# Attention scores read from the 32 rows of each head instead of from zero-padded keys of 128 rows

## What is computed

```python
N_HEADS = 16                      # hs = 128 // 16 = 8 features a head
Q, K, V = proj(Wq, bq), proj(Wk, bk), proj(Wv, bv)
Q, K = _apply_rope(Q, cos, sin), _apply_rope(K, cos, sin)
scores = jnp.einsum('bhqd,bhkd->bhqk', Q, K) * (1.0 / jnp.sqrt(hs))
scores = jnp.where(causal, scores, -10000000000.0)
...
```

## Time and profile before

| | |
|---|---|
| time, median of 3 runs | 1768.23 us (1767.26 to 1769.22) |
| time of the profiled execution | 1769.27 us |
| its span, first to last instruction | 1767.2 us |
| PE / DVE / ACT / POOL busy share of the span | 69% / 58% / 36% / 29% |
| mean granted TensorE clock, share of 2.4 GHz | 0.814 |

### The profile page before, as it was taken

How to read it: one execution, slowest core, us unless ns; L and a number is a source line. 1 busy time by engine, 2 the same in 40 slices (tenths; PEclk the granted TensorE clock), 3 DMA queues, 4 the chain that set the end, 5 groups by cost and what they waited for, 6 DMA issues and landing times. The chain is left out here.

```text
span 1767.2 us, 26688 instructions
## 1 busy us (share of the span) xinstructions
PE 1212.8 (69%) x9140; PEld 801.2 (45%) x9214; DVE 1021.9 (58%) x2340; ACT 629.5 (36%) x989; POOL 510.0 (29%) x571
## 2 busy tenths in 40 slices
PE   4625977959635059704888998899889997412991
PEld 2413856839524059702343443344434443311991
DVE  5855555655426136446777776777777770630662
ACT  4632221222111023201265664665566665001330
POOL 2434013040026747712003000300120000374772
PEclk9666988969755579955699998999999998555995
DMA  1439611020120133160000010001000100213325
GB/s 45 155 145 390 266 37 59 0 95 0 36 63 28 53 106 99 52 185 6 7 19 7 10 46 8 7 7 43 8 7 8 31 7 13 62 53 90 98 68 162
DMA packets 109057, 114.06 MB, mean 65 GB/s; under 512 B 8720, under 2 KB 90512, under 8 KB 108048
## 3 DMA queue, kind: packets, MB, share of 16 engines
q1 hardware_dynamic: 96608, 91.98, 16.5%
q0 software_dynamic: 9216, 19.02, 3.2%
q10 hardware_dynamic: 3120, 1.57, 0.3%
HBM read 49.34 MB, written 59.02 MB: 61 GB/s over the span
## 5 line engine op out<-in xcount | busy, mean ns | idle before, releaser
L1829 DVE TENSOR_REDUCE att_mx<-att_ps 128x1 f32<-128x512 f32 (+3 forms) x768 | 405.2, 555 | 146.9 <-PE att_ps L1722 111.3
L1603 ACT ACTIVATE att_prob<-att_ps 128x1024 f32<-128x1024 f32 (+3 forms) x384 | 300.3, 812 | 228.9 <-PE att_ps L1734 176.7
L1719 PE MATMUL att_ps<-att_kT,att_q1T 128*128 128x512 bf16 (+3 forms) x709 | 235.1, 344 | 50.5 <-DVE att_mx L1829 34.2
L1731 PE MATMUL att_ps<-att_q2T,att_kT 128*128 128x512 bf16 (+3 forms) x753 | 201.1, 331 | 3.2 <-ACT att_prob L1603 1.2
L1719 PEld LDWEIGHTS att_ps<-att_kT,att_q1T 128*128 128x128 bf16 x768 | 74.2, 98 | 259.1 <-DVE att_mx L1829 211.7
L978 POOL DMA_INDIRECT sides<-moe_ys,moe_back_i x160 | 153.2, 958 | 87.6 <-issue 47.3
L1745 PE MATMUL att_pso<-att_prob,att_v 128*32 128x512 f32 (+3 forms) x1536 | 163.9, 499 | 1.6
L972 POOL DMA_INDIRECT slots<-moe_rows,moe_place_i x128 | 123.2, 963 | 59.4 <-issue 38.4
L1499 POOL CAST att_qm_rows<-att_nm 128x32 bf16<-128x32 f32 x48 | 15.6, 324 | 395.8 <-DVE att_nm L1838 391.6
L1722 PE MATMUL att_ps<-att_mask,att_identb 128*128 128x128 bf16 x512 | 115.8, 228 | 2.3 <-DVE att_mx L1829 1.5
L1071 PE MATMUL moe_ps_t<-moe_ident,moe_xs 128*128 128x128 f32 x160 | 27.0, 290 | 115.2 <-DMA moe_xs<-slots 115.2
(11 more groups left out here) (283 smaller groups left out, 2439.5 us busy)
## 6 DMA issues: line engine op xcount, KB each, us to landing
slots<-fw_zeros SPq DMA_DIRECT2D x2, 5200.0 KB, 30.1
moe_xs<-slots SPq DMA_DIRECT2D x16, 650.0 KB, 4.9
sides<-fw_zeros SPq DMA_DIRECT2D x2, 4096.0 KB, 35.3
moe_side<-sides SPq DMA_DIRECT2D x16, 512.0 KB, 6.2
tok<-prep_tok SPq DMA_DIRECT2D x4, 1536.0 KB, 5.4
turned<-prep_tT SPq DMA_DIRECT2D x4, 1536.0 KB, 8.7
fw_tok<-tok SPq DMA_DIRECT2D x4, 1536.0 KB, 10.4
fw_Tkv<-turned SPq DMA_DIRECT2D x4, 1024.0 KB, 6.7
```

The lines of the kernel that those rows point to most:

```text
L1603: nc.scalar.activation(prob[(2 * n + pair) % 4][:, :, 0:size], ps2[pair][:, :, 0:size], ACT.Exp, scale=SCORE_SCALE).then_inc(exp_done, 1)
L1719: last = nc.tensor.matmul(out[:, 0:size], q1T[t % 2][:, j * P:(j + 1) * P], kT[t][h][:, 512 * c:512 * c + size], start=True, stop=not diag ...
L1731: last = nc.tensor.matmul(ps2[pair][:, h, 0:size], kT[t][2 * pair + h][:, i * P:(i + 1) * P], q2T[t % 2][:, first:first + size], start=Tru ...
L1829: nc.vector.reduce_max(mx[:, c, j, h:h + 1], ps1[(n * QUAD + h) % 2][:, 0:size], AX.X).then_inc(max_done, 1)
```

## The change

The padded tiles, their zeroing, `kT_all` and the four transfers go. `kT[t]` is one tile of 128 rows that ACT writes directly, and a score matmul names 32 partitions of it and of the queries, so that it is a matmul of 32 rows. In the max pass the heads come in the order 2, 0, 3, 1. In `exp_step` the two score matmuls of a pair come first, then the two masks. The mask matmuls keep their 128 rows.

```diff
-        kT = [[sb(f"kT{s}{h}", [P, SEQ], BF16) for h in range(QUAD)] for s in range(HEADS // QUAD)]
-        kT_all = sb("kT_all", [P, SEQ], BF16)
+        kT = [sb(f"kT{s}", [P, SEQ], BF16) for s in range(HEADS // QUAD)]
...
+        TURNS = (2, 0, 3, 1)
+
+        def head_rows(h):
+            return slice(32 * h, 32 * h + 32)
...
-            def place_keys(count, t):
-
-                wait(sp, misc_free, 1 + count + 1)
-                for h in range(QUAD):
-                    rows = slice(32 * h, 32 * h + 32)
-                    sp.dma_start(kT[t][h][rows, :], kT_all[rows, :]).then_inc(k_placed, 16)
...
-                    keys_from_misc(count, G + 2)
+                    from_misc(count, kT[(t + 2) % QUADS][:], psm_b)
...
-            def max_step(G, t, n, heads=range(QUAD)):
+            def max_step(G, t, n, turns=range(QUAD)):
...
+                    rows = head_rows(TURNS[i])
                     diagonal = P * (j + 1) == 512 * c + size
                     pe.wait_ge(max_done, u + 1)
-                    last = nc.tensor.matmul(out[:, 0:size], q1T[t % 2][:, j * P:(j + 1) * P], kT[t][h][:, 512 * c:512 * c + size],
+                    last = nc.tensor.matmul(out[:, 0:size], q1T[t % 2][rows, j * P:(j + 1) * P], kT[t][rows, 512 * c:512 * c + size],
                                             start=True, stop=not diagonal)
...
                 for h in range(2):
-                    last = nc.tensor.matmul(ps2[pair][:, h, 0:size], kT[t][2 * pair + h][:, i * P:(i + 1) * P], q2T[t % 2][:, first:first + size],
+                    rows = head_rows(2 * pair + h)
+                    last = nc.tensor.matmul(ps2[pair][:, h, 0:size], kT[t][rows, i * P:(i + 1) * P], q2T[t % 2][rows, first:first + size],
                                             start=True, stop=(i < 4 * c))
-                    if i >= 4 * c:
+                if i >= 4 * c:
+                    for h in range(2):
                         last = nc.tensor.matmul(ps2[pair][:, h, 0:P], identb[:], mask[:, 1], start=False, stop=True)
...
-                        pe.wait_ge(k_placed, (S.G + 3) * (QUAD * 16))
...
-                for h in range(QUAD):
-                    if n >= 2:
-                        nc.vector.memset(kT[n - 2][h][:], 0.0)
```

More of the change, by code:

```diff
@@ L1448, in _ @@
                         sp.dma_start(batch(x_out, b), res[:]).then_inc(x_stored, 16)
-                    place_keys(S.count("k"), (S.t + 2) % QUADS)
                 wait(sp, x_stored, b * 16 + 16)
                 sp.dma_start(res[:], batch(x_in, b + 1)).then_inc(res_loaded, 16)
-            for S in last_slots:
-                if S.more2:
-                    place_keys(S.count("k"), (S.t + 2) % QUADS)
             sp.wait_ge(out_done, 2 * BATCH)
@@ L1645, in _ @@
             stack_keys(2).then_inc(k_stacked, 1)
-            keys_from_misc(first_count("k"), None)
+            from_misc(first_count("k"), kT[0][:], psm_b)
             from_misc(first_count("q1"), q1T[0][:], psm_b)
-            keys_from_misc(first_count("k next"), 1)
+            from_misc(first_count("k next"), kT[1][:], psm_b)
             from_misc(first_count("q1 next"), q1T[1][:], psm_b)
@@ L1709, in produce @@
                     last.then_inc(misc_full, 1)
-            def max_step(G, t, n, heads=range(QUAD)):
+            def max_step(G, t, n, turns=range(QUAD)):
                 j, c = MAX_STEPS[n]
                 size = min(512, P * (j + 1) - 512 * c)
-                for h in heads:
-                    u = G * (STEPS * QUAD) + (n * QUAD + h)
-                    out = ps1[(n * QUAD + h) % 2]
+                for i in turns:
+                    u = G * (STEPS * QUAD) + (n * QUAD + i)
+                    out = ps1[(n * QUAD + i) % 2]
+                    rows = head_rows(TURNS[i])
                     diagonal = P * (j + 1) == 512 * c + size
                     pe.wait_ge(max_done, u + 1)
-                    last = nc.tensor.matmul(out[:, 0:size], q1T[t % 2][:, j * P:(j + 1) * P], kT[t][h][:, 512 * c:512 * c + size],
+                    last = nc.tensor.matmul(out[:, 0:size], q1T[t % 2][rows, j * P:(j + 1) * P], kT[t][rows, 512 * c:512 * c + size],
                                             start=True, stop=not diagonal)
@@ L1798, in _ @@
             pe.wait_ge(misc_free, 1 + first_count("q1") + 1)
-            pe.wait_ge(k_placed, QUAD * 16)
             for n in range(STEPS):
@@ L1823, in _, with maxima @@
         def _(dve):
-            def maxima(G, t, n, heads=range(QUAD)):
+            def maxima(G, t, n, turns=range(QUAD)):
                 j, c = MAX_STEPS[n]
                 size = min(512, P * (j + 1) - 512 * c)
-                for h in heads:
-                    dve.wait_ge(s1_done, G * (STEPS * QUAD) + (n * QUAD + h + 1))
-                    nc.vector.reduce_max(mx[:, c, j, h:h + 1], ps1[(n * QUAD + h) % 2][:, 0:size], AX.X).then_inc(max_done, 1)
+                for i in turns:
+                    h = TURNS[i]
+                    dve.wait_ge(s1_done, G * (STEPS * QUAD) + (n * QUAD + i + 1))
+                    nc.vector.reduce_max(mx[:, c, j, h:h + 1], ps1[(n * QUAD + i) % 2][:, 0:size], AX.X).then_inc(max_done, 1)
             def negate_maxima(G, first=False):
@@ L1924, in _ @@
             dve.wait_ge(weights_in, 7 * 16)
-            for n, use in enumerate(FIRST_USES[0:first_count("v0")]):
+            for use in FIRST_USES[0:first_count("v0")]:
                 consume(use, first_count(use), 0, 0)
-                for h in range(QUAD):
-                    if n >= 2:
-                        nc.vector.memset(kT[n - 2][h][:], 0.0)
             dve.drain()
```

3 lines of the change are left out of this document (1 added, 2 removed).

## The result

| | before | after |
|---|---|---|
| time, median | 1768.7 us (1767.3 to 1772.3) | 2021.2 us (1995.2 to 2366.6) |
| ratio | | 1.1385, 95% interval 1.1294 to 1.1477 |
| span of the profiled execution | 1767.2 us | 1993.2 us |
| granted TensorE clock over that span | 0.81 | 0.71 |
| first to last value step of the 16 slots | 611.5 us, clock 0.986 | 831.4 us, clock 0.699 |

The change is slower by 13.9%, and the forecast of 1829 us, range 1738 to 1882, does not hold it. One run after, 2366.6 us at a mean clock of 0.52, was disturbed: the median counts it, the ratio leaves it out. Of the 226 us between the two spans 220 lie between the first and the last value step.

A forecast was written before the change was run, and what follows sets the result against it. PE was taken to set the time in attention steps, DVE's reductions in others; +50 for eleven slots, +9 prep slots, +1 and +1 for the last two, start 0, made 1767.2 + 61 = 1828 of span, 1829 median, range 1738 to 1882.

The forecast's parts named there:

- the term that was to decide: Attention slots: switching between 32-row scores and 128-row work costs 0.12 us each, 90 more a slot; net +4.5 us a slot.
- A pair runs as one: Exp scores: two matmuls on different 32-row strips overlap and are counted as one matmul.
- n = 8 to 11: Intervals between value steps in a plain slot, ending at these n: 11 more changes each, +3.53 us for the four.
- The steps held to hang on DVE's reductions: Plain slot, n = 0, 4, 5 and 6: the DVE loop sets the time, so 15 more changes cost 0.
- The rivals without a price: Cheap row changes with overlap winning, 1730 us, chance 0.20; no overlap and no price, 1764 us, chance 0.05.
- Short falls: Slots: brief drops of PE's granted clock, worth 0 to 30 us, included in the range.
- a fall throughout: Rival: PE's clock falls to half throughout the slots, +370 us, 2200 us, chance 0.04.
- well under 0.99: Sign of being wrong: the slots' granted clock, 0.99 on average before, falling well below that.
- The last but one: The slot before the last: no maxima after n = 7, so only +1 us.
- the three prep slots: Slots of 50.55 us with PE busy 40.40, also waiting for DVE's other work: +3 us each, +9 together.
- n = 1, 2 and 3: Plain-slot intervals with 9, 6 and 9 more changes, put at +0.2 us each; PE's DVE wait absorbs cost at 1 and 3.
- The start: Before the slots: zeroing gone -2.1 at most, earlier first max turn -1.9, masked first max turns +4; together 0.

The follow-up runs named there:

- experiment 1: Changed kernel with blocks of matmuls put ahead of attention (one, two, four strips; alternating shapes; column tiles; full array): one strip 0.42 us a matmul, four strips 0.21 together.
- experiment 4: Changed kernel with each mask matmul issued four times, no change of shape added: ratio 1.1416 to the kernel before, slots 849.6 us.
- experiment 5: Kernel with padded and unpadded keys, only one pass reading 32 rows: ratio to the kernel before 1.0145 for exponentials alone, 1.0605 for maxima alone.

## Why the prediction was wrong

**What held.** The direction, and the term that was to decide, in its mechanism and, for the slots where it can be read, nearly in its size. A change of shape was put at 0.12 and costs 0.107, at either clock. A pair runs as one. The intervals at 2.4 GHz, for n = 8 to 11: predicted 4.08, 3.54, 3.66 and 3.97, measured 4.00, 3.40, 3.51 and 3.85; the difference is the 0.013 by which eleven changes were too dear. n = 7 was to be 3.84 and is 3.74. For n = 4 to 11 of like slots the growth is 3.5 us, predicted 3.9. The steps held to hang on DVE's reductions did so: n = 0, 4, 5 and 6 grew by -0.04, +0.05 to +0.14, +0.09 and +0.08, predicted 0. The rivals without a price (1730 and 1764) fell with the first fence of the timeline.

**The step that failed** is the clock: "Short falls are likelier and worth 0 to 30 us; they are in the range", with 0.04 for a fall throughout. The fall was neither short nor throughout: the mean clock of the slots is 0.70, which between the two levels is (1 - 0.70) / 0.5 = 0.6 of the stretch, some 500 us, at 1.2 GHz. The argument set against it, that value steps and masks, "more than half of what remains, keep the whole array", was never weighed: experiment 1 shows 32-row matmuls alone at half clock, and full-array ones held there by changes of shape between them; experiment 4 shows that it took three times as many masks more to come back to 0.92. A granted clock of the slots "well under 0.99" was named as a sign of being wrong, and it came. How much of the fall belongs to the strips and how much to the drains is not separated.

What it costs is an estimate. Where the changed kernel ran at a clock of 1.00, its intervals less those of like slots before give +0.46 to +0.62 at n = 3, the four values above for n = 0, 4, 5 and 6, +0.27 at n = 7, +0.51 to +0.60 at n = 8 (+0.17 in one slot), and +0.82, +0.78 and +0.79 at n = 9 to 11: 3.8 to 4.15 us together. The intervals of n = 1 and 2 never lay wholly at 1.00; the two halves of experiment 5 have +1.1 there. That is about 5 us a slot (4.5 predicted), 55 over eleven slots (50 predicted). The last but one gives up to 2.8 by the halves, and the three prep slots something between 0 and their whole growth of 10 to 12 each. So the price is 55 to 93 us, and the clock the other 127 to 165. A second reading points to the upper end for the clock: the plain slot takes 60.5 us at 1.2 GHz throughout (from 1588.07) where 34.26 + 5 would do at 2.4 GHz, a third of its time lost, and a third of 500 us is about 165. The prep slots' share is not settled.

| term | predicted, us | measured, us |
|---|---|---|
| slots, changes of shape less overlap | +61 | +55 to +93 (estimate) |
| slots, clock | 0 (0 to +30) | +127 to +165 (estimate) |
| slots together | +61 | +220 |
| all before the first value step and after the last | 0 | +6 |
| span | +61 | +226 |

**The price's own size.** The forecast's eleven changes at n = 8 to 11 were a little too dear; against that n = 1, 2 and 3, put at +0.2 each because PE waits there for DVE, cost more: +0.46 to +0.62 at n = 3, and +0.4 and +0.7 at n = 1 and 2 by the halves. A drain between a score and its mask delays the reduction that the next turn waits for, so a wait for DVE need not absorb it; that reason is argued and not isolated. The prep slots, put at +3 each, grew from 50.5, 51.8 and 50.6 us to 62.6, 62.3 and 62.1, at clocks of 0.69 to 0.72; what of that is price and what clock is not separated.

**The start.** "Together 0": the first maximum turn starts at 831.64, directly behind the copy of the queries (830.57 + 1.02), where before 2 us lay between the earlier trace rows; that gain is real. The turn itself is later, 831.64 against 830.23, because the stage begins 3.9 us later (its first matmul at 795.88 in place of 791.97), before anything that was changed has run; counted from there it comes 2.5 us earlier, 1.9 by the transfers and 0.6 by the zeroings, which had been put at up to 2.1. Against it the first maxima, up to the first value step, take 883.20 - 831.64 = 51.6 us in place of 876.21 - 830.23 = 46.0, +5.6 where +4 was put; the granted clock there is 0.50 in place of 0.60, so part of it is clock. The +6 of the table is so 3.9 that the change did not cause, -2.5, +5.6, and -1.0 behind the last value step.

**The numbers.** The price came near its forecast, and one term put at nothing, the clock, makes most of the miss of 165 us on the span (1993.2 against 1828). The range ended at 1882 because the case "throughout" was priced at 2200 and held to be rare, with nothing between it and 30 us. A clock with two levels gives everything in between: in the slots of the changed kernel it stayed at 1.2 GHz for stretches of a few us up to a hundred (1585.73 to 1688.13).

## What to carry to other kernels

A matmul on fewer rows does not hold the array for a shorter time; it pays only where matmuls on other strips run at the same moment, all four if it can be, and where few changes to 128-row work lie between. Count the changes: each is 0.107 us, the time of 256 columns at 2.4 GHz. And when a change takes work off the array while PE stays on the critical path, price the whole stage at 1.2 GHz as a case of its own, and what lies between; zero rows that seem wasted may be what holds the clock. Before grouping work to feed PE better, look who consumes it: here ACT was waited for as soon as its scores came late.

## What the hardware showed that I had not expected

- PE busy for 29.00 of 29.00 us with 512-column matmuls on one 32-row strip, back to back, at a granted clock of 0.50; the same on two strips; four strips 1.00.
- The same half clock without any strip: full-array matmuls of 128 columns with a change of shape between each two stayed at 0.50 from 987.67 to 1041, and the clock rose once the changes were gone.
- More work, hardly more time: 154 us of masks added, the stretch longer by 16.5 us, clock 0.70 to 0.92.
- The price of a change of shape does not scale with the array's clock: 0.107 us at 2.4 GHz, 0.108 at 1.2 GHz.
- Four strips of 512 columns took 0.21 us together, no longer than one matmul over all rows.
